# Fused attention and gated feed-forward on one core: places for split values, first queries in a rotary key's bank, a later copy of x, joined late transposes, last tokens tile by tile

## The chip, the cores and the metric

The kernel runs on 1 core of one Trainium2 chip. The metric is the device time of one execution in microseconds (us). The kernel before has a median of 2392.24 us over 3 runs (2391.26 to 2392.67).

## What is computed

One transformer layer on x with shape (2, 1024, 512). Attention has 32 query heads and 8 key and value heads of 128; keys are half rotary (from `Wkr`) and half made from a latent (`Wdk`, then `Wupk`), values come from the latent too (`Wupv`). The feed-forward part has 1376 hidden columns and weights packed in 4 bits.

```python
q = (x @ Wq.T).reshape(...)            # 32 heads, rotary
k_r = rotary(x @ Wkr.T)
c_kv = x @ Wdk.T
k_c, v = c_kv @ Wupk.T, c_kv @ Wupv.T  # 8 heads
attn = softmax(mask(q @ k.T / sqrt(128)))
x = layernorm(x + (attn @ v) @ Wo.T)
h = silu(x @ W1.T) * (x @ W3.T)
out = layernorm(x + h @ W2.T)
```

## The kernel before, in words

Every number is split into a high part (fp32r) and the low rest, and each product is three matmuls: high by high, high by low, low by high (`three_pass`, L262). Tokens come in four blocks of 512 (NBLK = 4, END = 3).

Phase A makes keys and values. For each block, TensorE makes four rotary key groups (RG + m), four latent key groups (NG + n) and eight value groups (VG + n) of 12 matmuls each, in a ring of eight PSUM banks (`a_bank`, L395). ScalarE takes the high part out of the bank (L991 for keys, L996 for values), VectorE the low part (L1246, L1251), and SyncE (SP) stores both (L617 `a_store_k`, L622 `a_store_v`). Rotary keys are turned by VectorE, and GpSimd (POOL) makes their low part (L892). Keys have four places in SBUF (`a_ks`), values two (`a_vs`); a place is used again when its store has landed (`a_k_out`, `a_v_out`). SP issues every transfer of the kernel, in one order written by hand: the parts of x of each block (L609), a copy of all of x to y in DRAM after block 0 (L820), keys and values of head group 0 in the third block (L667, L671), parts of x for the first queries (L674), sine and cosine (L830, L831), and so on.

Between A and B, for h in 0 to 3: late value group h (of the fourth block, h < V_LATE = 3), then queries h. The queries go into `banks[h % 2]`, which are the banks of latent keys 2 and 3. For each head ScalarE copies the two halves of the product swapped (L1032, L1033), POOL multiplies by sine (L897), VectorE by cosine (L1268), VectorE adds (L1275), ScalarE takes the high part (L1040) and VectorE, for these four, the low part (L1506).

Phase B has 16 turns (one for each batch and key head; turn 0 is "first", 1 to 14 a loop, 15 "last"), and a turn has 32 steps (CELLS), one for each query tile i = c // 4 and head h = c % 4. In step s TensorE computes the scores of cell s, transposes the normalised scores of cell s - 3 (LAG), and does a share of the "fill" (L77 to L95): queries for the next turn (q0, q1), products with the values (pv), with the output weights (wo) and, in turn 0, the late values 3 to 7 (va). `Plan` spreads the fill over the steps by the room of each (ROOM). Cells of query tiles 4 to 7 are transposed in two pieces, the first of four key tiles into one bank, the rest into the other (`pieces`, L55; `transposes`, L1610). A piece may be transposed when the scores are normalised (`norm_done`) and when VectorE has copied out the piece that was in this bank (`pt_lo`). In steps from 16 on the order on TensorE is scores, fill, piece 0, fill, piece 1, fill (PE_ORDER, L114), with the fill cut 1 : 1.25 : 1 (SHARES, L119; `turn_of`, L1790). ScalarE normalises (L1067), takes high parts (L1082) and exponentials (L1061) in the order of ACT_ORDER; VectorE adds the mask and finds the maximum (L1286) and takes low parts (L1304). The sum with x goes through y in DRAM (`load_y`, `store_y`, L676 to L682).

Phase C is the feed-forward part, four blocks. For each of the 11 hidden tiles f, TensorE does 24 up products (gate and up, L1638) and 12 down products (L1670), three for each of the four token tiles, which sum in four banks over all f. ScalarE takes silu (L1125) and the high part (L1128), VectorE the gate product (L1372) and the low part (L1378), into one of two places (`c_hs`). In the last block the down products of the last two tiles are ordered by token tile (`c_last_downs`, L1680); then VectorE adds the residual tile by tile (L1391) and takes statistics (L286), and one variance, one root (L305) and one chain of small steps (L312 to L320) serve the four tiles, before four scalings (L325) and three stores (L863).

```python
1826            for h in range(GQ):
1827                if h < V_LATE:
1828                    a_group(END, VG + h, a_values(END, h))
1829                if h < 2:
1830                    pe.wait_ge(a_bank_free, a_count(END, NG + 2 + h) + a_FREE0)
1831                else:
1832                    pe.wait_ge(q_cos, h - 1)
1833                queries(0, 0, h, h % 2, 0, products("q0", h))
```

Of the kernel before, what the change touches and what calls it, by code (L numbers as in the profile page):

```python
# [22 lines left out]
F32R = mybir.dt.float32r  # L23
# [95 lines left out]
SHARES = ((1,), (0, 1), (1, 1.25, 1))  # L119

# [151 lines left out]
class LayerNorm:  # L272
# [30 lines left out]
    def square_root(self, act, g):  # L303
        act.wait_ge(self.asked, g + 1)
        self.nc.scalar.activation(self.sd[:], self.var[:], ACT.Sqrt).then_inc(self.sqrt_done, 1)  # L305

    def reciprocal_root(self, dve, g):

        nc, var, sd, rs, tmp = self.nc, self.var[:], self.sd[:], self.rs[:], self.tmp[:]
# [23 lines left out]
def layer(nc, x, xT, wqT, wkrT, wdkT, wupkT, wupvT, woT, w13p, s13p, w2p, s2p, cosT, sinT, shifts,  # L333
# [5 lines left out]
    with ExitStack() as ctx:  # L339
# [22 lines left out]
        a_vs = at(164 * K, "a_vs", [P, 2, 4, 2, HD], F32R)  # L362
# [56 lines left out]
        a_v_out = [sem("a_v_out0"), sem("a_v_out1")]  # L419
# [167 lines left out]

        blocks_of_y = y_d.rearrange("b (h i) p d -> (b h) i p d", i=4)
# [4 lines left out]
        def _(sp):  # L593
# [26 lines left out]
            def a_store_v(t, n):  # L620
# [4 lines left out]
                    words(a_vs[:, n % 2]).rearrange("p g l d -> p g (l d)")).then_inc(a_v_out[n % 2], 16)  # L625

            def a_block_of(t):
# [150 lines left out]
            def turn_of(it, turn):  # L778
                for step in steps_of(turn):
# [40 lines left out]
            sp.dma_start(y_d.rearrange("b i p d -> (b i p) d"), x.rearrange("b s d -> (b s) d")).then_inc(a_y_out, 16)  # L820
# [11 lines left out]
            for n in range(8):  # L832
                a_store_k(END, n)
# [1082 lines left out]
```

## Time and profile before

| | |
|---|---|
| median of 3 runs | 2392.24 us |
| the profiled execution | 2391.44 us |
| its span, first to last instruction | 2389.7 us |
| mean granted TensorE clock | 0.997 |
| TensorE (PE) busy | 2366.3 us, 99% |
| weight loads (PEld) | 1988.7 us, 83% |
| ScalarE (ACT) | 1619.6 us, 68% |
| VectorE (DVE) | 1421.9 us, 60% |
| GpSimd (POOL) | 577.2 us, 24% |

Times in rows are counted from the start of the span. A matmul's duration in a row (0.39 us for 512 columns) is longer than the distance from one start to the next, because matmuls are pipelined; work is therefore counted from start to start. A row of the timeline merges neighbours of one kind: start, length, engine, line, operation, output and inputs, count, and in brackets the engine's idle time before it and what ended that. A few matmul records are missing from a trace, so a count can be one short.

### The profile page before, as it was taken

What the parts mean: (1) busy time and instruction counts of PE and PEld (TensorE: products, weight loads), DVE (VectorE), ACT (ScalarE), POOL (GpSimd) and SP (SyncE); (2) the same over time, 40 slices, a digit from 0 to 9 for tenths busy, and PEclk for the clock granted to TensorE, in tenths of its full rate; (3) what the DMA queues carried; (4) which work ended last, traced back from release to release, by engine and by line L of the source; (5) the groups of instructions that cost most, each with busy time, mean ns of one, the idle gap of its engine ahead of it and who ended that gap; (6) DMA issues with size and microseconds to landing.
All of it is one profiled execution on the core that took longest, in us unless ns stands there. A gap on an engine that the chain in (4) does not pass through costs nothing.

```text
span 2389.7 us, 40886 instructions
## 1 busy us (share of the span) xinstructions
PE 2366.3 (99%) x11999; PEld 1988.7 (83%) x11999; DVE 1421.9 (60%) x3781; ACT 1619.6 (68%) x3220; POOL 577.2 (24%) x451
## 2 busy tenths in 40 slices
PE   9998999999999999999999999999999999999998
PEld 8887888888888888888888888888888888888886
DVE  5334666676767676766667676766676665242332
ACT  4223878788888888887878888888888885122211
POOL 2101323233332323232323333232323220000000
PEclk9999999999999999999999999999999999999999
DMA  6787344444453544344444435354434445321110
GB/s 220 280 297 275 132 145 133 134 140 145 134 170 109 174 136 149 127 145 136 137 140 140 142 131 167 113 176 127 159 126 145 132 137 206 123 71 36 53 36 18
DMA packets 133256, 340.26 MB, mean 142 GB/s; under 512 B 13328, under 2 KB 30736, under 8 KB 122640
## 3 DMA queue, kind: packets, MB, share of 16 engines
q1 hardware_dynamic: 133200, 339.53, 42.5%
q8 instruction: 32, 0.52, 0.1%
q14 instruction: 24, 0.20, 0.0%
HBM read 232.00 MB, written 111.67 MB: 144 GB/s over the span
## 4 chain that ended last, share of the span: by engine, by line
PE 87%; DMA 1%; issue 1%; ACT 1%; DVE 1%; POOL 0%; SPq 0%; DVEq 0%; ACTq 0%; POOLq 0%
PE b_ps L267 43%; PE b_sps L267 28%; PE b_tps L1615 10%; PE b_ps L1674 3%; PE b_tps L1674 2%; DMA v_d<-a_vs 0%; DMA k_d<-a_ks 0%; ACT b_pt L1082 0%; DMA b_kt<-k_d 0%; PE b_sps L1624 0%; ACT b_sc L1067 0%; ACT b_sc L1061 0%; DMA y_d<-b_ys 0%; POOL b_sw L897 0%; DVE b_pt L1304 0%
## 5 line engine op out<-in xcount | busy, mean ns | idle before, releaser
L1304 DVE TENSOR_TENSOR b_pt<-b_tps,b_pt 128x512 fp32r<-128x512 f32 (+3 forms) x768 | 426.6, 556 | 302.2 <-ACT b_pt L1082 297.8
L267 PE MATMUL b_sps<-b_kt,b_qs 128*128 128x512 f32 (+4 forms) x2304 | 497.3, 343 | 1.3 <-DVE b_nmax L1286 1.0
L1067 ACT ACTIVATE b_sc<-b_sc,b_rinv 128x896 f32<-128x896 f32 (+7 forms) x512 | 396.1, 774 | 105.3 <-DVE b_rinv L1294 98.6
L267 PEld LDWEIGHTS b_sps<-b_kt,b_qs 128*128 128x128 f32 x2304 | 403.1, 188 | 57.8 <-issue 1.9
L267 PE MATMUL b_ps<-b_xs,b_wq 128*128 128x512 f32 x1536 | 443.1, 408 | 5.6 <-DVE a_ks L1246 5.6
L1082 ACT ACTIVATE b_pt<-b_tps 128x512 fp32r<-128x512 f32 (+3 forms) x768 | 367.5, 479 | 117.5 <-PE b_tps L1615 115.9
L267 PE MATMUL b_ps<-b_pt,b_vt 128*128 128x512 f32 x1584 | 436.2, 403 | 0.3 <-DVE b_ys L1315 0.3
L267 PE MATMUL b_ps<-b_wo,b_ot 128*128 128x512 f32 x1536 | 423.9, 405 | 0.1
L1061 ACT ACTIVATE b_sc<-b_sc,b_nmax 128x896 f32<-128x896 f32 (+7 forms) x512 | 395.4, 772 | 38.2 <-DVE b_nmax L1286 35.1
L1286 DVE CUSTOM_DVE_ANT_0 b_sc<-b_sps,b_mask 128x896 f32<-128x896 f32 (+7 forms) x512 | 386.4, 755 | 15.5 <-PE b_sps L267 15.4
L1615 PE MATMUL b_tps<-b_ident,b_sc 128*128 128x128 f32 x2304 | 374.5, 272 | 4.5 <-ACT b_sc L1067 2.9
L1615 PEld LDWEIGHTS b_tps<-b_ident,b_sc 128*128 128x128 f32 x2304 | 291.4, 140 | 80.2 <-issue 5.3
L267 PEld LDWEIGHTS b_ps<-b_pt,b_vt 128*128 128x128 f32 x1584 | 284.3, 188 | 49.0 <-DVE b_ys L1315 0.5
L267 PEld LDWEIGHTS b_ps<-b_xs,b_wq 128*128 128x128 f32 x1536 | 275.3, 190 | 51.6 <-DVE a_ks L1246 6.1
L267 PEld LDWEIGHTS b_ps<-b_wo,b_ot 128*128 128x128 f32 x1536 | 270.8, 189 | 43.5 <-DVE b_ys L1315 0.3
L897 POOL TENSOR_TENSOR b_sw<-b_sw,b_sin 128x512 f32<-128x512 f32 x128 | 165.7, 1295 | 374.9 <-ACT b_sw L1033 373.5
L901 POOL TENSOR_TENSOR b_qs<-b_qf,b_qs 128x512 fp32r<-128x512 f32 x124 | 160.3, 1293 | 395.0 <-ACT b_qs L1040 395.0
L267 PE MATMUL b_sps<-c_xs,c_up 128*128 128x512 f32 (+3 forms) x1056 | 247.5, 390 | 0.0
L267 PEld LDWEIGHTS b_sps<-c_xs,c_up 128*128 128x128 f32 (+1 forms) x1056 | 195.2, 185 | 43.7
L1372 DVE TENSOR_TENSOR c_hb<-b_sps,c_hb 128x512 f32<-128x512 f32 (+1 forms) x44 | 30.4, 691 | 193.4 <-PE b_sps L267 186.9
L1268 DVE TENSOR_TENSOR b_qf<-b_ps,b_cos 128x512 f32<-128x512 f32 x128 | 88.5, 691 | 90.8 <-ACT b_sw L1033 48.9
L910 POOL TENSOR_TENSOR b_wo<-b_wraw,b_wo 128x512 fp32r<-128x512 f32 x64 | 82.9, 1295 | 229.3 <-ACT b_wo L1055 229.3
(169 smaller groups left out, 2250.0 us busy)
## 6 DMA issues: line engine op xcount, KB each, us to landing
b_xs<-xs_d SPq DMA_DIRECT2D x32, 2048.0 KB, 9.3
b_ys<-y_d SPq DMA_DIRECT2D x128, 256.0 KB, 2.7
y_d<-b_ys SPq DMA_DIRECT2D x128, 256.0 KB, 3.0
b_wraw<-in_wqT SPq DMA_DIRECT2D x64, 256.0 KB, 2.8
k_d<-a_ks SPq DMA_DIRECT2D x32, 512.0 KB, 4.9
v_d<-a_vs SPq DMA_DIRECT2D x32, 512.0 KB, 3.2
b_kt<-k_d SPq DMA_DIRECT2D x64, 256.0 KB, 4.6
b_vt<-v_d SPq DMA_DIRECT2D x16, 1024.0 KB, 4.8
```

Of the source, the lines that this page charges most:

```text
L267: ins = nc.tensor.matmul(out, *every[n], start=(n == 0), stop=(n == len(every) - 1))
L897: nc.gpsimd.tensor_tensor(sw[:], sw[:], sinq[:, blk * TB:blk * TB + TB], ALU.mult).then_inc(sin_done, 1)
L901: nc.gpsimd.tensor_tensor(qs[:, blk, h, LO], qf[:], qs[:, blk, h, HI], ALU.subtract).then_inc(q_lo, 1)
L910: nc.gpsimd.tensor_tensor(wo[:, h, LO], wraw[:, h % 2], wo[:, h, HI], ALU.subtract).then_inc(w_lo, 1)
L1061: nc.scalar.activation(sc[:, slot, 0:w], sc[:, slot, 0:w], ACT.Exp, bias=nmax[:, slot:slot + 1], scale=-1.0, accum_out=rsum[:, slot:slot + ...
L1067: nc.scalar.activation(sc[:, slot, 0:w], sc[:, slot, 0:w], ACT.Copy, scale=rinv[:, slot:slot + 1])\
L1082: nc.scalar.activation(pt[:, u % PT_UNITS, HI, 0:nj, h * P:(h + 1) * P], tps[n % 2][:, 0:nj], ACT.Copy)\
L1268: nc.vector.tensor_tensor(qf[:], banks[bk], cosq[:, blk * TB:blk * TB + TB], ALU.mult)\
L1286: nc.vector.tensor_tensor_reduce(out=like_banks(sc[:, slot, 0:w], i), in0=both_banks(sps[c % 2], i), in1=like_banks(mask[:, S - w:S], i), ...
L1304: nc.vector.tensor_tensor(pt[:, u, LO, 0:nj, h * P:(h + 1) * P], tps[n % 2][:, 0:nj], pt[:, u, HI, 0:nj, h * P:(h + 1) * P], ALU.subtract) ...
L1615: last = nc.tensor.transpose(tps[n % 2][:, j], sc[:, c % S_RING, (j0 + j) * P:(j0 + j + 1) * P], ident[:])
L1674: last = nc.tensor.matmul(c_y[t], c_hs[0:w, f % 2, a, t * P:(t + 1) * P], c_w2[f][b][0:w], start=(f == 0 and k == 0), stop=(f == FT - 1 an ...
```

## The change

Values get four places, two of them where phase B has the values of a head group (8 and 12 KB); the first two query groups use the bank of rotary key 3 and come ahead of the late values; the copy of x to y is cut to the tiles that turn 0 does not read (nine of sixteen) and moves to step 13 of turn 0, which reads x itself; several transfers of SP move. From step 22 on the two pieces of a cell are transposed one right after the other. The last feed-forward block does all up products, then the down products token tile by token tile, with the hidden parts kept in the place of the up weights already used, and each token tile is normalised and stored by itself.

```diff
+JOINED = 22
+JOINED_ORDER, JOINED_SHARES = ("scores", "fill", 0, 1, "fill"), (1, 2.25)
...
+    def variance_of_tile(self, dve, g, t):
+        nc = self.nc
+        nc.vector.bn_stats(self.stats[:, t], self.tile(t)).then_inc(self.st, 1)
+        dve.wait_ge(self.st, 9 * g + 2 * t + 1)
+        nc.vector.bn_aggr(self.mv[:, t], self.stats[:, t]).then_inc(self.st, 1)
+        dve.wait_ge(self.st, 9 * g + 2 * t + 2)
+        nc.vector.tensor_scalar(self.var[:, t:t + 1], self.mv[:, t, 1:2], EPS, None, ALU.add).then_inc(self.asked, 1)
...
-    def square_root(self, act, g):
+    def square_root(self, act, g, t=0, width=4):
-    def reciprocal_root(self, dve, g):
+    def reciprocal_root(self, dve, g, t=0, width=4):
...
-        a_vs = at(164 * K, "a_vs", [P, 2, 4, 2, HD], F32R)
+        a_vs = [at(kb * K, f"a_vs{n}", [P, 4, 2, HD], F32R) for n, kb in enumerate((164, 168, 8, 12))]
...
+        def a_v_slot(t, n):
+            return n % 4 if t < END or n < 4 else n % 2
+        def a_v_uses(t, n):
+            return 2 * t + n // 4 if t < END or n < 4 else 2 * END + 1 + (n - 4) // 2
+        V_USES = [1 + max(a_v_uses(END, n) for n in range(8) if a_v_slot(END, n) == k) for k in range(4)]
+        Q_BANK = (3, 3, 0, 1)
...
+        y_rest, x_rest = (w[(QT - 1) * P:] for w in (y_d.rearrange("b i p d -> (b i p) d"),
+                                                     x.rearrange("b s d -> (b s) d")))
+        def c_h(n, f):
+            if type(n) is int and n == END:
+                return c_up[f][:].rearrange("q l m k c -> q (l m k c)")[:, 0:2 * TB].rearrange("q (l t) -> q l t", l=2)
+            return c_hs[:, f % 2]
...
             def a_block_of(t):
-                if t == END - 1:
-                    sp.wait_ge(a_fused, a_made(3, 3))
-                    for slot in range(4):
-                        sp.wait_ge(a_k_out[slot], 16 * 2 * 2)
-                    load_k(0)
                 for n in range(8):
-                    if t == END - 1 and n == 4:
-                        for p in range(2):
-                            sp.wait_ge(a_v_out[p], 16 * 4 * 2 + a_OUT0)
-                        load_v(0)
+                    if t == END - 1 and n == 7:
+                        sp.wait_ge(a_mm, a_count(END - 1, VG + 7) + a_MM0)
+                        sp.wait_ge(a_xs_out, 16 * END + a_OUT0)
+                        load_xs(0, 0)
                     a_store_v(t, n)
...
+                first = type(it) is int and it == 0
-                sp.dma_start(ys[:, i % 2], y_d[it // KV, i]).then_inc(y_in[i % 2], 16)
+                sp.dma_start(ys[:, i % 2], x_tiles[i] if first else y_d[it // KV, i]).then_inc(y_in[i % 2], 16)
...
+                    if step == 0 and turn == "loop":
+                        sp.wait_ge(a_y_out, 16)
+                    if turn == "first" and step == 5:
+                        for p in range(4):
+                            sp.wait_ge(a_v_out[p], 16 * (V_USES[p] if p >= 2 else 4) + a_OUT0)
+                        load_v(0)
+                    if turn == "first" and step == 6:
+                        a_store_x(END)
+                    if turn == "first" and step == 13:
+                        sp.dma_start(y_rest, x_rest).then_inc(a_y_out, 16)
...
             a_block_of(0)
-            sp.dma_start(y_d.rearrange("b i p d -> (b i p) d"), x.rearrange("b s d -> (b s) d")).then_inc(a_y_out, 16)
...
-            sp.wait_ge(a_mm, a_count(END - 1, VG + 7) + a_MM0)
-            sp.wait_ge(a_xs_out, 16 * END + a_OUT0)
-            load_xs(0, 0)
             sp.wait_ge(a_x_lo, END + a_XLO0)
-            sp.dma_start(sinq[:], sinT).then_inc(tab_in, 16)
-            sp.dma_start(cosq[:], cosT).then_inc(tab_in, 16)
             for n in range(8):
+                if n == 2:
+                    sp.dma_start(sinq[:], sinT).then_inc(tab_in, 16)
+                    sp.dma_start(cosq[:], cosT).then_inc(tab_in, 16)
+                if n == 4:
+                    load_k(0)
                 a_store_k(END, n)
             for n in range(V_LATE):
                 a_store_v(END, n)
             sp.wait_ge(q_mm, 4)
             load_xs(0, 1)
-            a_store_x(END)
...
-            for t, to in ((0, 2), (2, 3), (3, 4)):
+            for t in range(4):
+                sp.wait_ge(norm2.done, 4 * END + t + 1)
+                sp.dma_start(out[END, t], c_x1[:, t]).then_inc(c_o_out, 16)
...
             # ScalarE, between A and B (VectorE alike: queries, then the late value)
             for h in range(GQ):
+                swap_q(0, 0, h, Q_BANK[h])
+                hi_q(0, 0, h)
                 if h < V_LATE:
                     a_v_hi(END, h, a_bank[(VG + h) % a_RING])
-                swap_q(0, 0, h, h % 2)
-                hi_q(0, 0, h)
...
             def c_last_sum():
                 for t in range(4):
                     c_residual(END, (t,))
+                    dve.wait_ge(c_z_done, 4 * END + t + 1 + Z0)
+                    norm2.variance_of_tile(dve, END, t)
+                    norm2.reciprocal_root(dve, END, t, 1)
+                    norm2.scale_tiles((t,))
...
+            def c_last_block():
+                for index, (kind, what) in list(enumerate(ITEMS["last"]))[1:]:
+                    c_item(END, index, kind, what, "last")
+                pe.wait_ge(c_z_done, 4 * END + Z0)
+                for t in range(4):
+                    for f in range(FT):
+                        if t == 0:
+                            pe.wait_ge(c_h_lo, FT * END + f + 1 + HLO0)
+                        c_down_products(END, f, t)
...
-                    shares = cut(parts, SHARES[len(ts)])
-                    for job in (0, 1, "scores") if step == 0 else PE_ORDER[part_of(step)]:
+                    joined = step >= JOINED and len(ts) == 2
+                    shares = cut(parts, JOINED_SHARES if joined else SHARES[len(ts)])
+                    order = JOINED_ORDER if joined else PE_ORDER[part_of(step)]
+                    for job in (0, 1, "scores") if step == 0 else order:
...
             for h in range(GQ):
+                if h == 0:
+                    pe.wait_ge(a_bank_free, a_count(END, RG + 3) + a_FREE0)
+                elif h == 1:
+                    pe.wait_ge(q_cos, 1)
+                else:
+                    pe.wait_ge(a_bank_free, a_count(END, NG + h) + a_FREE0)
+                queries(0, 0, h, Q_BANK[h], 0, products("q0", h))
                 if h < V_LATE:
                     a_group(END, VG + h, a_values(END, h))
```

## Rows read from the trace of the kernel before

**Rows 1.** Windows of TensorE: us, busy us (matmuls), granted clock, DMA share, GB/s

```profile
194.00:222.00 28.00, 22.36 (x87) 0.88 0.62 226
222.00:245.00 23.00, 18.89 (x94) 1.00 0.82 290
245.00:2380.00 2135.00, 2132.59 (x10977) 1.00 0.39 128
```

**Rows 2.** List of waits: engine and line <- what it waited for: us, times, longest

```profile
ACT a_vs L996 <- DMA v_d<-a_vs: 39.2, 13, 11.0
...
PE b_tps L1615 <- ACT b_sc L1067: 2.9, 1, 2.9
```

**Rows 3.** Timeline of the opening, TensorE and VectorE

```profile
194.47 2.88 PE L267 MATMUL b_sps<-a_wupv,a_xe 128*128 128x512 f32 x12
...
202.99 5.49 PE L267 MATMUL b_ps<-b_xs,b_wq 128*128 128x512 f32 x12 [5.64 <-DVE a_ks L1246]
...
209.76 0.69 DVE L1268 TENSOR_TENSOR b_qf<-b_ps,b_cos 128x512 f32<-128x512 f32 x1 [4.93 <-ACT b_sw L1033]
...
222.07 0.39 PE L267 MATMUL b_ps<-a_wupv_hi,a_xe 128*128 128x512 f32 x1
```

**Rows 4.** Chain of waits in the opening: start, us, what

```profile
192.83 8.77 DMA k_d<-a_ks
...
223.55 0.60 ACT b_sw L1032
...
230.23 9.45 DMA v_d<-a_vs
```

**Rows 5.** DMA issues by kind: out<-in, count, KB each, median us to landing

```profile
b_xs<-xs_d SPq DMA_DIRECT2D x32, 2048.0 KB, 9.3
...
y_d<-in_x SPq DMA_DIRECT2D x1, 16.1
```

**Rows 6.** Timeline of TensorE, steps 3 and 4 of turn 0

```profile
234.06 1.32 PE L267 MATMUL b_ps<-b_xs,b_wq 128*128 128x512 f32 x5
```

**Rows 7.** Timeline of TensorE in the feed-forward blocks

```profile
2092.96 1.04 PE L1624 MATMUL b_sps<-b_ident,c_yb 128*128 128x128 f32 x8
...
2099.38 0.60 PE L1624 MATMUL b_sps<-b_ident,c_yb 128*128 128x128 f32 x4
...
2150.71 1.52 PE L1674 MATMUL b_ps<-c_w,c_hs 128*128 128x512 f32 x6
2152.07 1.03 PE L1624 MATMUL b_sps<-b_ident,c_yb 128*128 128x128 f32 x8
...
2158.43 1.52 PE L1674 MATMUL b_tps<-c_w,c_hs 128*128 128x512 f32 x6
```

**Rows 8.** Timeline of a turn, steps 24, 29 and 30: TensorE, and VectorE's copy

```profile
1184.04 1.39 PE L267 MATMUL b_sps<-b_kt,b_qs 128*128 128x448 f32 x6
...
1188.94 0.56 PE L267 MATMUL b_sps<-b_kt,b_qs 128*128 128x448 f32 x2
...
1207.48 1.53 PE L267 MATMUL b_sps<-b_kt,b_qs 128*128 128x512 f32 x6
...
1209.42 0.56 DVE L1304 TENSOR_TENSOR b_pt<-b_tps,b_pt 128x384 fp32r<-128x384 f32 x1 [1.08 <-ACT b_pt L1082]
...
1209.77 0.60 PE L1615 MATMUL b_tps<-b_ident,b_sc 128*128 128x128 f32 x4
...
1212.62 1.54 PE L267 MATMUL b_sps<-b_kt,b_qs 128*128 128x512 f32 x6
```

**Rows 9.** Timeline of the tail

```profile
2377.03 2.94 PE L1674 MATMUL b_ps<-c_w,c_hs 128*128 128x512 f32 x12
...
2380.01 0.69 DVE L1391 TENSOR_TENSOR c_x<-b_ps,c_x 128x512 f32<-128x512 f32 x1
...
2384.07 1.91 DVE L325 TENSOR_SCALAR c_x<-c_x,c_n_mv,c_n_rs 128x512 f32<-128x512 f32 x4
```

**Rows 10.** Stores of y, line 682: us from issue to landing, least, median, most

```profile
DMA to landing us min/median/max: 2.0/3.0/17.1
```

More of the change, by code:

```diff
@@ L418, in layer @@
         a_xs_out, a_y_out = sem("a_xs_out"), sem("a_y_out")
-        a_v_out = [sem("a_v_out0"), sem("a_v_out1")]
+        a_v_out = [sem(f"a_v_out{n}") for n in range(4)]
         tab_in, masked = sem("b_tab_in"), sem("b_masked")
@@ L824, in _ @@
                 a_block_of(t)
[L826 to L828 removed]
             sp.wait_ge(a_x_lo, END + a_XLO0)
[L830 to L831 removed]
+            sp.wait_ge(a_fused, a_made(3, 3))
+            for slot in range(4):
+                sp.wait_ge(a_k_out[slot], 16 * 2 * 2)
             for n in range(8):
+                if n == 2:
[3 more added lines that the diff above has]
+                    load_k(0)
                 a_store_k(END, n)
@@ L860, in _ @@
             c_block_io(END, True)
-            for t, to in ((0, 2), (2, 3), (3, 4)):
-                sp.wait_ge(norm2.done, 4 * END + to)
-                sp.dma_start(out[END, t:to].rearrange("i p d -> p i d"), c_x1[:, t:to]).then_inc(c_o_out, 16)
+            for t in range(4):
+                sp.wait_ge(norm2.done, 4 * END + t + 1)
+                sp.dma_start(out[END, t], c_x1[:, t]).then_inc(c_o_out, 16)
             sp.wait_ge(c_x1_out, 16 * NBLK)
-            sp.wait_ge(c_o_out, 16 * (NBLK + 2))
+            sp.wait_ge(c_o_out, 16 * (NBLK + 3))
         @block.gpsimd
@@ L949, in _ @@
             act.sem_inc(a_xs_out, a_OUT0)
-            act.sem_inc(a_v_out[0], a_OUT0)
-            act.sem_inc(a_v_out[1], a_OUT0)
+            for p in range(4):
+                act.sem_inc(a_v_out[p], a_OUT0)
             act.sem_inc(y_out[0], YO0)
@@ L1250, in a_v_lo @@
                 dve.wait_ge(a_part_hi, a_count(t, VG + n))
-                nc.vector.tensor_tensor(a_vs[:, n % 2, :, LO, :], ps.rearrange("p (g d) -> p g d", g=4),
-                                        a_vs[:, n % 2, :, HI, :], ALU.subtract).then_inc(a_bank_free, 1)
+                place = a_vs[a_v_slot(t, n)]
+                nc.vector.tensor_tensor(place[:, :, LO, :], ps.rearrange("p (g d) -> p g d", g=4),
+                                        place[:, :, HI, :], ALU.subtract).then_inc(a_bank_free, 1)
             def a_block_of(t):
@@ L1385, in c_residual @@
                         dve.wait_ge(c_x1_in, 16 * n + 16)
-                    if t < 3:
+                    if type(n) is int and n == END:
+                        dve.wait_ge(c_y_done, 3 * n + t + 1)
+                    elif t < 3:
                         dve.wait_ge(c_y_done, 3 * n + t + 1)
@@ L1701, in c_block_of @@
                         c_item(n, index, kind, what, place)
-                        if kind == "f" and (f < FT - 2 - (place == "last") or not todo):
+                        if kind == "f" and (f < FT - 2 or not todo):
                             break
@@ L1709, in c_block_of @@
                         pe.wait_ge(c_ab_free, PER)
-                    if f == FT - 1 and place != "last":
+                    if f == FT - 1:
                         c_item(n + 1, 0, "f", 0)
-                    if place == "last" and f == FT - 2:
-                        c_last_downs(n)
-                        break
                     if place != "first":
@@ L1826, in _ @@
             for h in range(GQ):
+                if h == 0:
[5 more added lines that the diff above has]
+                queries(0, 0, h, Q_BANK[h], 0, products("q0", h))
                 if h < V_LATE:
                     a_group(END, VG + h, a_values(END, h))
-                if h < 2:
-                    pe.wait_ge(a_bank_free, a_count(END, NG + 2 + h) + a_FREE0)
-                else:
-                    pe.wait_ge(q_cos, h - 1)
-                queries(0, 0, h, h % 2, 0, products("q0", h))
             turns(pe, turn_of)
@@ L1837, in _ @@
                 c_block_of(n, "next")
-            c_block_of(END, "last")
+            c_last_block()
 def kernel(L0_attn_hidden_states, L0_attn_Wq, L0_attn_Wkr, L0_attn_Wdk, L0_attn_Wupk, L0_attn_Wupv, L0_attn_Wo,
```

62 lines of the change are left out of this document (24 added, 38 removed).

## The prediction

> **What bounds the kernel now.** The windows of TensorE come first: from 245 to 2380 us it idles 2.4 of 2135 us. Between 194 and 245 us it idles 5.6 and 4.1 us [rows 1], and after 2380 us it has nothing left. So time can come from three places alone: this opening, the 9.7 us of the tail, and the spacing of TensorE's instructions in between. The list of waits names who was late: ScalarE waited 39.2 us for stores of values to land, and 2.9 us of TensorE stand against ScalarE's normalised scores [rows 2]. The timeline of the opening shows the first hole and its echo: a value group at 194.47 us, the first queries only at 202.99 us, behind VectorE's low parts of the keys, and these 12 products take 5.49 us where 12 take 2.7 elsewhere: after the idle stretch the granted clock had fallen to the lower of its two levels, 1.2 instead of 2.4 GHz. The late values of turn 0 begin at 222.07 us [rows 3]. The chain of waits says what was last: a key store that took 8.77 us to land, ScalarE's copy of queries 3 only at 223.55 us, a value store of 9.45 us [rows 4].
>
> All durations are of the profiled execution: span 2389.7 us, its own time 2391.44 us, 0.8 us under the median of 2392.24 us. I take the differences from the median.
>
> **Opening: 13.0 us before new costs.** Why does a store of 512 KB take 9 us, when one of 256 KB has a median of 3.0 [rows 10]? All transfers stand in SP's one list, and the large ones block it: the copy of x to y took 16.1 us, each 2 MB load of x parts 9.3 us [rows 5]. The change takes the 4 MB copy away from 87 us, moves the values of head group 0 (1 MB) from 172.8 us to step 5 and its keys (1 MB) behind the four rotary key stores, issues the 2 MB of x parts ahead of the third block's last value store and not at 184 us, and gives values four places for two. Up to 194 us TensorE has nothing to gain from that, since it is not in the list of waits there. But VectorE is no longer held by late values , so I expect rotary keys and their stores some 5 us sooner, and ScalarE through with the keys at about 195.5 us, just behind the last latent key group (194.47 us), instead of 203.5 us. Sine and cosine (1 MB, by the rate of rows 5 about 4.5 us) now stand ahead of the last two rotary stores; the 5 us cover them.
>
> The queries: the first product no longer needs a latent key's bank, only that of the fourth rotary key, which VectorE has left by then, so queries 0 go at 194.47 us. Queries 1 use the same bank and wait for the cosine of queries 0. Queries 0 now end about 208.5 and their cosine at 209.76 + 0.69 = 210.45 us [rows 3], 2.0 us later; the value group put between lasts 2.7 us, 0.7 us more. Seven groups of 12 at 2.72 us are 19.04 us; they took 222.07 - 194.47 = 27.60 us [rows 3]. Gain 8.6 us, the clock's 2.8 us among them.
>
> Next, ScalarE began on queries 3 at 223.55 us, 1.5 us after they were done, since it still had queries 2 in hand, and the mask and the third cell's scores followed late [rows 4]. With value group 2 between them this goes: 1.5 us. Late value 4 then waited for a store of 9.45 us that stood behind 2 MB of x in and 2 MB out [rows 4]; its new place was last used by value 0, and the store of x moves to step 6: the 2.9 us of TensorE go [rows 2]. Sum 8.6 + 1.5 + 2.9 = 13.0 us.
>
> **New queueing: costs 0.8 us (0 to 3).** The second load of x parts, issued right behind queries 3, takes 9.3 us [rows 5] and has a value store just ahead of it now; its first user comes about 10.5 us after queries 3 (234.06 - 222.07 is 12.0, less 1.5) [rows 6]: 0 to 0.5 us late. At step 5 SP waits until the places at 8 and 12 KB are stored, then loads the values over them; behind stand the store of x, value stores, and output weights wanted at step 11, some 12 us on. Value 7's place waits for the store of value 5 behind 3 MB: up to 1 us. The copy of the nine tiles left (2.4 MB) at step 13 takes 16.1 x 9/16 = 9 us and stands ahead of four loads of query weights and 2 MB of x parts; the third of these weights may come 2.5 us late for ScalarE. All exposed: 3 us. I take 0.8, near the lower end, as ScalarE has slack in these steps and TensorE follows it two steps behind. Net 12.2 us.
>
> **Transposes side by side: 6.0 us (0 to 10).** Six products of 512 columns last 1.36 us (2150.71 to 2152.07), 0.2267 us each [rows 7]; one transpose 0.1085 from start to start. Step 29 of a turn has 6 scores, 13 fills and 4 + 3 transposes: 19 x 0.2267 + 7 x 0.1085 = 5.07 us, and took 5.14 (1207.48 to 1212.62). Step 24 has 6 scores of 448 columns (in proportion 0.1984 each), 13 fills, 6 transposes: 4.79 us, and took 4.90 (1184.04 to 1188.94) [rows 8]. So two blocks of transposes cost 0.07 and 0.11 us beyond their parts, 0.09 in the mean. One block of eight, in the feed-forward part, with 24 products: 8 x 0.1085 + 24 x 0.2267 = 6.31 us, and took 6.36 (2152.07 to 2158.43) [rows 7]. A block costs 0.05 us, whatever its length. The change makes one block of two in ten steps (22 to 31) of 16 turns: 160 x 0.04 = 6.4 us, of which I take 6.0. Ends: another block of eight cost 0.11 us (2092.96 to 2099.38 is 6.42) [rows 7], no less than two blocks, so 0; and 0.11 - 0.05 = 0.06 us per step gives 10.
>
> Here a rule speaks against the change. The Trainium skill (TensorE: Matmul & The Clock Gate, section Back-to-back issue gap) gives a matmul's spacing as its columns over the clock plus 2.5 ns, with no price for a change of kind; by it the sum would be 6 us smaller. The trace does not agree: 227 ns for 512 columns against 216 ns by the rule, and 0.05 us per block.
>
> A joined second block also needs its bank copied out by VectorE since the step before: that ends at 1209.42 + 0.56 = 1209.98 us, and the block would start at 1209.77 + 4 x 0.1085 = 1210.20 us [rows 8]. The slack is 0.2 us in this step, the tightest that I found; cost 0.
>
> **Tail: 3.1 us (2.5 to 3.5).** The last block does its gate and up products in one run, then the down products tile by tile (33 each, 7.5 us): as many products as before. Sums, normalisation and stores of tiles 0 to 2 lie beside TensorE's work, 7.5 us for a chain of about 4. Now: products end at 2379.97 us, one sum at 2380.01, two statistics, one variance for four tiles, four scalings from 2384.07 to 2385.98, stores, end at 2389.70: 9.7 us [rows 9]. Then: sum 0.7, statistics 0.7, two small steps 0.4, root 0.3, five small steps 1.1 and one scaling 0.54 make 3.8 us; a 256 KB store lands in 2.0 us at best and 3.0 at the median [rows 10], here alone in the list, so 2.3; and 0.5 to the end: 6.6 us. Hidden parts live in the weights already used, so ScalarE waits for no down product; a gate of 0.7 us each 5.4 us leaves VectorE room for the block before.
>
> **Sum.** 12.2 + 6.0 + 3.1 = 21.3 us: 2392.24 - 21.3 = 2370.9, forecast 2371 us (span 2368.4).
>
> **Rivals.** (1) Grouping transposes gives nothing: for it the block at 2092.96 us, against it the one at 2152.07; the sum without its 6 us is 2377 us. Chance 0.17. (This is what the Trainium skill's rule above would do.) (2) In the opening one wait takes the other's place: rotary key stores still land 8.8 us late, ScalarE copies queries 0 at 203.5 us, and queries 1, bound to the same bank, start at 205.4 instead of 199.9 us; with the clock's fall 5.5 + 2.7 = 8.2 us are lost again: 2379 us. For it: sine, cosine and keys are still loaded in this stretch; against: the copy, the values and the 2 MB of x parts are out of the way by then. Chance 0.13. (3) Slower: joined second blocks wait for VectorE's copy. The slack is 0.2 us [rows 8]; beyond it 0.1 us in each of 160 steps costs 16 us, and from 0.1 us the 15 us of the rest are gone; at 0.25 us it is 40 - 15 = 25 us slower, 2417 us. For it: VectorE waits 1.08 us for ScalarE before that copy; against: ScalarE takes this piece behind its exponential in either order. Chance 0.03. (4) The early transfers are no cause of the holes and the regrouping does nothing: 2389 us by the tail alone, 0.04.
>
> **Numbers.** Forecast 0.63. Range 2366 (ten for the regrouping, no new cost) to 2379 us (rival 2 in full). A measurement tells about 0.2% (4.8 us) from no change: faster 0.94, same 0.03, slower 0.03.
>
> **What would show it.** Opening: no hole over 1 us from 190 to 245 us, granted clock 1.0 there, first late group near 213.5 us, ScalarE's wait for value stores under 15 us; wrong if TensorE waits for b_qf L1268. Turns 0.4 us shorter, step 29 at 5.11 us, no wait of transposes for b_pt L1304. Step 13: a wait for b_wraw under 3 us, ScalarE's alone. Tail: 6.6 us from last product to end. The forecast falls if the time between 245 and 2380 us keeps its length, or the half clock is seen again in the opening.

## The result, and the profile after

The changed kernel takes 2375.57 us (median of 4 runs, 2374.07 to 2376.76) beside 2391.75 us for the kernel of before (4 runs, 2390.52 to 2392.67): ratio 0.9932, 95% interval 0.9915 to 0.995. That is 16.2 us where 21.3 were forecast; the range of 2366 to 2379 us holds it. The profiled execution has a span of 2374.0 us (its own time 2375.78), 15.7 us less than before.

The windows of TensorE in the trace after (us, busy us and matmuls, granted clock, DMA share, GB/s):

```profile
194.00:222.00 28.00, 27.87 (x129) 1.00 0.71 243
222.00:245.00 23.00, 20.68 (x101) 0.93 0.75 260
245.00:280.00 35.00, 34.51 (x183) 1.00 0.68 228
280.00:1900.00 1620.00, 1618.89 (x8585) 1.00 0.42 141
1900.00:2020.00 120.00, 117.62 (x607) 1.00 0.47 171
```

The first line answers to the first of [rows 1]: the hole is gone and the clock stays up. The second idles 2.3 us where it idled 4.1, but the clock is below full there, and the two losses together are as large as before. The timeline of TensorE, and the chain of waits (start, us, what), tell both halves:

```profile
193.57 2.88 PE L269 MATMUL b_sps<-b_xs,b_wq 128*128 128x512 f32 x12
...
209.89 2.88 PE L269 MATMUL b_ps<-b_xs,b_wq 128*128 128x512 f32 x12
212.61 0.39 PE L269 MATMUL b_ps<-a_wupv_hi,a_xe 128*128 128x512 f32 x1
...
239.29 0.55 PE L1658 MATMUL b_tps<-b_ident,b_sc 128*128 128x128 f32 x3 [2.32 <-ACT b_sc L1108]
...
327.20 0.98 PE L269 MATMUL b_sps<-b_kt,b_qs 128*128 128x256 f32 x6
```

```profile
226.60 11.45 DMA v_d<-a_vs
...
238.13 0.60 ACT a_vs L1037
...
250.52 10.97 DMA b_wraw<-in_wqT
```

Seven groups take 212.61 - 193.57 = 19.04 us, and the first late group starts 9.5 us sooner than at 222.07 us [rows 3]. But the first scores of turn 1, at 336.60 us before and 327.20 us now, come only 9.4 us sooner: turn 0 gains nothing. The store of late value 5 lands 11.45 us after its issue, behind 1 MB of values in and 2 MB of x out. Late value 7 uses its place, ScalarE stands there, and normalised scores wait behind it: 2.32 us of TensorE. In the 4 us after that the granted clock is 0.57:

```profile
236.00:240.00 4.00, 1.68 (x10) 1.00 0.96 349
240.00:244.00 4.00, 4.00 (x13) 0.57 0.01 3
```

0.43 x 4 = 1.7 us more. The prediction had named both as signs against it: a hole over 1 us between 190 and 245 us, and the half clock seen again in the opening. In the list of waits (0 to 300 us) ScalarE's 39.2 us for value stores [rows 2] are down to 2.9 us, and there is a new wait for query weights, behind the copy that now stands at step 13:

```profile
ACT b_wq L1087 <- DMA b_wraw<-in_wqT: 3.2, 3, 2.3
ACT a_vs L1037 <- DMA v_d<-a_vs: 2.9, 1, 2.9
```

Steps 24 and 29 of a turn [rows 8] now take 4.86 us (1171.96 to 1176.82) and 5.13 us (1195.26 to 1200.39), where they took 4.90 and 5.14:

```profile
1171.96 1.38 PE L269 MATMUL b_sps<-b_kt,b_qs 128*128 128x448 f32 x6
...
1176.82 1.38 PE L269 MATMUL b_sps<-b_kt,b_qs 128*128 128x448 f32 x6
```

```profile
1195.26 1.52 PE L269 MATMUL b_sps<-b_kt,b_qs 128*128 128x512 f32 x6
...
1200.39 1.53 PE L269 MATMUL b_sps<-b_kt,b_qs 128*128 128x512 f32 x6
```

The tail [rows 9]: the last products end where the group of 17 does, 2363.77 + 4.03 = 2367.80 us, and the span at 2374.0, so 6.2 us for 9.7.

```profile
2363.77 4.03 PE L1717 MATMUL b_ps<-c_w,c_up 128*128 128x512 f32 x17
...
2367.84 0.69 DVE L1437 TENSOR_TENSOR c_x<-b_ps,c_x 128x512 f32<-128x512 f32 x1 [3.83 <-PE b_ps L1717]
...
2370.97 0.55 DVE L339 TENSOR_SCALAR c_x<-c_x,c_n_mv,c_n_rs 128x512 f32<-128x512 f32 x1
```

So the 15.7 us of the spans are 9.4 up to turn 1, 2.4 from there to the feed-forward part, and 3.9 in it and in the tail. Forecast were 12.2, 6.0 and 3.1.

### The profile page after: what moved, and what is told of

It is laid out like the page before. It is cut to its first block, busy times and chain, and to the rows that moved or that the text cites. A ratio compares the mean times of both kernels' runs of the same rounds, so it can differ in the third digit from the quotient of the medians.

```text
span 2374.0 us, 40892 instructions
## 1 busy us (share of the span) xinstructions
PE 2359.8 (99%) x11999; PEld 1994.7 (84%) x11999; DVE 1425.0 (60%) x3797; ACT 1619.1 (68%) x3223; POOL 577.5 (24%) x451
## 4 chain that ended last, share of the span: by engine, by line
PE 96%; DMA 2%; ACT 1%; DVE 1%; issue 0%; POOL 0%; SPq 0%; ACTq 0%; DVEq 0%; POOLq 0%
PE b_ps L269 45%; PE b_sps L269 32%; PE b_tps L1658 10%; PE b_tps L1717 3%; PE b_ps L1717 3%; PE b_tps L269 2%; DMA v_d<-a_vs 1%; DMA b_kt<-k_d 0%; DMA b_wraw<-in_wqT 0%; ACT b_sc L1102 0%; ACT b_sc L1108 0%; PE b_tps L1579 0%; PE b_sps L1667 0%; ACT b_pt L1123 0%; DVE b_sc L1330 0%
## 5 line engine op out<-in xcount | busy, mean ns | idle before, releaser
L1348 DVE TENSOR_TENSOR b_pt<-b_tps,b_pt 128x512 fp32r<-128x512 f32 (+3 forms) x768 | 426.4, 555 | 304.5 <-ACT b_pt L1123 300.3
L269 PE MATMUL b_ps<-b_pt,b_vt 128*128 128x512 f32 x1584 | 423.9, 399 | 0.3 <-DVE b_ys L1359 0.3
L269 PE MATMUL b_ps<-b_xs,b_wq 128*128 128x512 f32 x1512 | 418.7, 402 | 0.0
L269 PE MATMUL b_ps<-b_wo,b_ot 128*128 128x512 f32 x1536 | 415.6, 403 | 0.0
L1658 PE MATMUL b_tps<-b_ident,b_sc 128*128 128x128 f32 x2304 | 349.9, 273 | 4.5 <-ACT b_sc L1108 2.3
L1658 PEld LDWEIGHTS b_tps<-b_ident,b_sc 128*128 128x128 f32 x2304 | 282.8, 140 | 61.2 <-issue 5.3
```

Of the source, the lines that this page charges most:

```text
L269: ins = nc.tensor.matmul(out, *every[n], start=(n == 0), stop=(n == len(every) - 1))
L1348: nc.vector.tensor_tensor(pt[:, u, LO, 0:nj, h * P:(h + 1) * P], tps[n % 2][:, 0:nj], pt[:, u, HI, 0:nj, h * P:(h + 1) * P], ALU.subtract) ...
L1658: last = nc.tensor.transpose(tps[n % 2][:, j], sc[:, c % S_RING, (j0 + j) * P:(j0 + j + 1) * P], ident[:])
```

## The experiments

Each time stands beside the kernel of before on the same chip: 2391.58 us (21 runs) for e1 to e4, 2390.04 (9 runs) for e5 to e8, 2389.97 (15 runs) for e9 to e11, 2391.93 (7 runs) for e12. Single executions of one kernel spread over 0.4 to 5.4 us, and an interval of the ratio is 4 to 8 us wide in all, where most parts that are tried here are worth 1 to 4 us. So differences between medians decide little by themselves, and the profiles decide.

**e1: the old order of transposes.**

```diff
-JOINED = 22
+JOINED = 99
```

> The changed kernel with the transposes of steps 22 to 31 in the old order and the old shares. Theory A (read from the two traces: a turn became 0.25 to 0.3 us shorter, of which the last four steps save 0.04 us each and the steps before them less, and the last turn gained about 1 us of small holes): slower than the changed kernel by 3 to 4 us, 2379.1 us, with turns back at 111.15 us. Theory B (the forecast, 0.04 us in each of 160 steps): slower by 6.0 us, 2381.6 us. Theory C (regrouping gives nothing, the turns became shorter for another reason): 2375.6 us and turns still at 110.9 us.

2377.59 us, ratio 0.9945 (0.9932 to 0.9959): 2.0 us slower than the changed kernel, 2.2 if each is taken from its own kernel of before. That is below A's 3 to 4 and B's 6, though these medians alone don't exclude either.

**e3: the new order alone, in the kernel of before** (the same lines of the diff, without the rest).

> The kernel of before with the regrouped transposes alone (steps 22 to 31 of every turn). Theory A: 4 us faster than before, 2387.8 us, turns 0.25 to 0.3 us shorter, small holes of about 1 us in the last turn. Theory B (the forecast): 6.0 us faster, 2385.8 us. Theory C: no gain, 2391.8 us.

2389.67 us (11 runs), ratio 0.9992 (0.9983 to 1.0001): 1.9 us faster, not clear of no change by the times. I then split each turn in the four traces at its first scores and its last. In the 13 turns after turn 1 the part between them takes 103.12 to 103.21 us before and 102.93 to 102.98 us after; with order back it is 103.10 to 103.21, with order alone 102.93 to 102.99. So regrouping is worth 0.20 us a turn, and that is sharp. What is left of a turn, from its last scores to the next turn's first, scatters from 7.8 to 8.7 us in all four kernels, and was once 9.6. And in the last turn regrouping costs 0.7 us of idle time, as the windows from 1900 us show, of before, of order alone, and of order back:

```profile
1900.00:2020.00 120.00, 118.28 (x619) 1.00 0.41 142
```

```profile
1900.00:2020.00 120.00, 117.56 (x612) 1.00 0.42 150
```

```profile
1900.00:2020.00 120.00, 118.21 (x609) 1.00 0.47 175
```

There transposes wait for VectorE's copy, 1.9 us in 5 waits (L1348) for 1.3 us in 4 before: the mechanism of rival 3, in one turn with short steps. From its first scores to its last this turn takes 93.42 us in the changed kernel and 92.51 before. 15 x 0.20 - 0.9 = 2.1 us, beside 1.9 and 2.0 measured.

**e6: regrouped in steps 28 to 31 only, and not in the last turn.**

```diff
-JOINED = 22
+JOINED = 28
...
-                    joined = step >= JOINED and len(ts) == 2
+                    joined = step >= JOINED and len(ts) == 2 and turn != "last"
```

> The changed kernel with the regrouped transposes in steps 28 to 31 only and not in the last turn. Theory A (only the last four steps save anything, 0.04 us each and the turn's start 0.03; in the last turn joined second blocks wait for VectorE, 0.7 us in all): from first to last scores a turn takes 102.95 to 103.00 us as in the changed kernel, the last turn's TensorE idle time between 1900 and 2020 us falls from 2.4 to 1.7 us, 0.3 to 0.7 us faster than the changed kernel, 2375 us. Theory B (all ten steps save alike, 0.02 us each): a turn takes 103.07 us, 1 us slower in all, 2376.6 us.

2376.82 us, ratio 0.9942 (0.9928 to 0.9956): 1.2 us slower than the changed kernel, 3.0 if each is taken from its own kernel of before, so the times can't choose between the theories. Between its first and last scores a turn now takes 103.05 to 103.11 us in 11 of 13 turns (two were longer): B. Four steps save some 0.07 us of 0.20, as they would if all ten save 0.02 alike. The last turn's idle time did fall to 1.75 us.

**e4: the new last block alone**, in the kernel of before.

> The kernel of before with the new last block alone (gate and up products in one run, down products tile by tile, each tile normalised and stored by itself). Theory A (the tail alone changes): from the last product to the end 6.2 to 6.6 us in place of 9.7, 3.1 to 3.5 us faster, 2388.5 us. Theory B (the order of the last block also costs or gives TensorE time): the sum of the block's products differs from before by over 0.5 us and the total gain lies outside 2.5 to 4 us.

2387.51 us (11 runs), ratio 0.9984 (0.9975 to 0.9993): 4.1 us faster, a little over A's 3.5 and over B's bound of 4, but the interval reaches from 1.7 to 6.0 us. In the trace it is A: its last product ends at 2380.45 us of a span of 2386.6, 6.15 us. From the last wait of the last turn to the last product it is 376.54 us, 376.94 before and 376.56 in the changed kernel: 3.5 us of tail and 0.4 us ahead of it.

**e2: the store of x parts behind value 5's.**

```diff
-                    if turn == "first" and step == 6:
-                        a_store_x(END)
...
                             a_store_v(END, a)
+                            if a == 5:
+                                a_store_x(END)
```

> The changed kernel with the 2 MB store of x parts behind the store of late value 5 and no longer ahead of it. Theory A (late value 7 waited for the store of value 5, which stood behind values in and x out, and TensorE lost 2.3 us there and about 1.6 us of half clock after it): the store of value 5 lands near 232.5 us in place of 237.8, the hole at 236.7 us is gone, the granted clock stays 1.0 from 194 to 262 us, and the time is 3.9 us shorter, 2371.7 us. Theory B (the hole only moves: the output weights and the store of value 6 stand behind the 2 MB instead, and ScalarE waits for them before it copies output weights): no gain within 1 us, 2375.6 us, with a hole of about 2 us between 238 and 250 us.

2374.88 us, ratio 0.993 (0.9917 to 0.9944): 0.7 us faster than the changed kernel (0.5 beside before), not 3.9. The hole and the half clock are gone, and so far A is right, though value 5's store landed at 234.88 us and not near 232.5; but 1.3 us more is lost in the next window:

```profile
222.00:245.00 23.00, 22.94 (x120) 1.00 0.75 274
245.00:280.00 35.00, 33.22 (x175) 1.00 0.67 222
```

```profile
ACT b_wq L1087 <- DMA b_wraw<-in_wqT: 2.7, 2, 1.5
```

TensorE arrives sooner at the query weights, which stand behind the copy of nine tiles. That is B in kind, in another place than it said. And at turn 1 TensorE waits 1.7 us for the keys, of which more below.

Theory A's 3.9 us was also taken from one execution. e1, e5 and e6 issue the same transfers in the same order up to there, and their profiles show the hole at 1.49 to 1.57 us with no half clock, but more idle time in the next window. These are e5's:

```profile
222.00:245.00 23.00, 21.51 (x113) 1.00 0.75 274
245.00:280.00 35.00, 33.22 (x177) 1.00 0.67 223
```

In all, e1, e5 and e6 idle 3.0 to 3.3 us between 222 and 280 us, e2 1.8 us.

**e7: the copy back at 87 us, on top of e2.**

```diff
-                    if turn == "first" and step == 13:
-                        sp.dma_start(y_rest, x_rest).then_inc(a_y_out, 16)
...
             a_block_of(0)
+            sp.dma_start(y_rest, x_rest).then_inc(a_y_out, 16)
             load_wq(0, 2)
```

> The kernel with the store of x parts later, and with the copy of nine tiles of x to y back behind the first block's stores (87 us) in place of step 13. Theory A (the copy at step 13 makes query weights late: TensorE idle 1.8 us between 245 and 280 us): these holes go, the opening to 194 us is no longer, 1 to 1.8 us faster than that kernel, 2373.5 us. Theory B (the early copy was what made the rotary key stores late at 190 us): a hole of some us comes back at 194 to 205 us and the time is 3 to 8 us longer, 2378 us or more. Theory C (the holes come from the 2 MB of x parts and not from the copy): no change within 0.5 us.

2370.72 us (2369.89 to 2371.0), ratio 0.9918 (0.9904 to 0.9931): 19.3 us faster than before, where e2 had 16.7 (the intervals of the two overlap). In the trace, A:

```profile
222.00:245.00 23.00, 23.00 (x120) 1.00 0.77 280
245.00:280.00 35.00, 35.00 (x191) 1.00 0.49 162
```

The 1.8 us of e2's idle time are gone, and up to 280 us no wait over 0.2 us is left. The move to step 13 cost time and brought none; nine tiles at 87 us don't disturb the opening.

**e8: banks and order of the first queries as before.**

```diff
-        Q_BANK = (3, 3, 0, 1)
+        Q_BANK = (0, 1, 0, 1)
```

and each late value group ahead of its queries again, on the three engines.

> The changed kernel with the first queries back in the banks of before, (0, 1, 0, 1), and each of the three late value groups again ahead of its queries; the four places for values and the moved transfers stay. Theory A (the transfers alone held the keys up; the latent keys now leave their banks at 193.6 and 195.6 us): no hole at 194 to 205 us, first late group of turn 0 still near 213 us, at most 1.5 us slower by the third cell, 2375.6 to 2377 us. Theory B (the bank and the order are what removes the hole): a hole of 3 to 6 us comes back at 197 us with half the clock behind it, 2380 to 2384 us.

2376.81 us (4 runs), ratio 0.9942 (0.9927 to 0.9957). A: no hole at 197 us. The one place up to 222 us where it waits is the third cell's scores, 0.95 us (as in the trace of before) against my 1.5:

```profile
220.20 0.59 PE L269 MATMUL b_sps<-b_kt,b_qs 128*128 128x256 f32 x3 [0.95 <-DVE b_nmax L1330]
```

By the medians e8 is 1.2 us slower than the changed kernel, and 3.0 if each is taken from its own kernel of before, against A's 1.5 at most. The profiled execution was the slowest of its four (2380.9 us); it has the hole behind value 5's store too (2.47 us up to 241.78, half the clock after it) and one of 1.56 us at 272 us. How much of that belongs to the banks isn't shown.

**e10: two places for values**, on top of e7.

```diff
-            return n % 4 if t < END or n < 4 else n % 2
+            return n % 2
...
-            return 2 * t + n // 4 if t < END or n < 4 else 2 * END + 1 + (n - 4) // 2
+            return 4 * t + n // 2
```

> The kernel with store of x parts later and the copy early, but two places for values in place of four; all transfers stay where the change put them. Theory A (the order of the transfers alone makes the stores short: with nothing of 1 to 4 MB ahead of them they land in about 3 us, and two places are enough): ScalarE's waits for value stores under 3 us between 100 and 200 us, no hole over 1 us at 194 to 210 us, within 1 us of the kernel with four places, 2370.7 us. Theory B (the places are what frees ScalarE and VectorE for the rotary keys): waits for value stores of 10 us and more, the hole comes back at about 196 us and half a clock behind it, 5 to 9 us slower, 2376 to 2380 us.

2371.36 us (4 runs), ratio 0.9921 (0.9905 to 0.9936): 18.6 us faster than before. A in the time, half A in the waits: ScalarE waits four times what A allowed, and TensorE does not wait for it.

```profile
ACT a_vs L1036 <- DMA v_d<-a_vs: 12.3, 6, 5.0
```

**e12: keys and values of group 0 back in the third block**, on top of e10: the two loads and their waits at the places that the change took them from.

> The kernel with two places for values, the copy early and the store of x parts later, but with the keys (1 MB) and the values (1 MB) of head group 0 again loaded in the third block's stores, as before the change; the 2 MB of x parts stay ahead of that block's last value store. Theory A (these two loads, ahead of value stores that ScalarE waits for, are what made the whole list late up to 200 us): ScalarE waits for value stores 25 us and more between 100 and 222 us, the x parts are issued near 182 us in place of 172.3, and TensorE idles 4 to 6 us near 197 us with half a clock behind it, 6 to 8 us slower than with two places alone, 2377.5 to 2379.5 us. Theory B (the x parts' place and the order of the rotary stores carry it): no hole over 1 us at 194 to 210 us, within 1 us of 2371.4 us.

2370.78 us (4 runs, 2369.59 to 2374.73; the slowest is the profiled one), ratio 0.9909 (0.9892 to 0.9925): 21.2 us faster than before. My theory A falls: ScalarE waits 26.8 us for value stores, as it said, and TensorE has no hole up to 280 us.

```profile
ACT a_vs L1036 <- DMA v_d<-a_vs: 26.8, 12, 5.2
...
ACT a_xs L1011 <- DMA a_xraw<-in_xT: 2.7, 1, 2.7
```

The same two lines of the kernel of before, in the same window of 100 to 222 us:

```profile
ACT a_vs L996 <- DMA v_d<-a_vs: 34.2, 12, 11.0
...
ACT a_xs L971 <- DMA a_xraw<-in_xT: 8.4, 1, 8.4
```

The last line points at what is left: ScalarE got the next block's x at 108.5 us before, 8.4 us late, and gets it at 103.1 us here, 2.7 us late. The copy at 87 us was 4 MB and took 16.1 us [rows 5]; here it is 2304 KB and takes some 11 us, and seven tiles of x go to their users straight from the input:

```profile
y_d<-in_x SPq DMA_DIRECT2D x1, 2304.0 KB, 11.6
```

(This row is e7's, with the copy in the same place.) The last value store of the second block was issued at 139.1 us before, at 131.9 us in e12; the 2 MB of x parts at 184.1 and 175.4 us. So the list ran 5 to 9 us late from the copy on, and the x parts ahead of a value store keep it short at the end.

The wait that made the first hole was one for stores of keys, though, not of values. A latent key's high part needs the place of a rotary key, and the stores of the four rotary keys stood behind the 2 MB of x parts and behind sine and cosine. ScalarE's first latent key of this block, before and in e12:

```profile
199.06 0.60 ACT L991 ACTIVATE a_ks<-b_tps 128x512 fp32r<-128x512 f32 x1 [7.02 <-DMA k_d<-a_ks]
```

```profile
188.65 0.60 ACT L1031 ACTIVATE a_ks<-b_tps 128x512 fp32r<-128x512 f32 x1 [1.24 <-DMA k_d<-a_ks]
```

The first rotary store was issued at 188.93 us before and took 10.1 us; in e12 it goes at 182.81 us and takes 5.8. Three parts of the change are in every kernel without the hole, then: the smaller copy, the x parts ahead of a value store, and sine and cosine behind the first two rotary stores. Which of the three does most wasn't tried, and stays open.

**e5: three products more between the last scores of a turn and the next keys.**

```diff
-        11, 7]
+        8, 7]
```

(the room of step 30; step 31 takes what is over)

> The changed kernel with three products moved from step 30 to step 31 of a turn, so that 0.68 us more of TensorE's work lies between the last scores of a turn and the first of the next. Theory A (each turn start waits for the four loads of keys: in the changed kernel the stretch from the last scores to the first of the next turn took 7.81 to 8.67 us, mean 8.02, while without a wait it would take 7.81): the stretch becomes 8.49 us in all turns but the worst, the rest of the turn 102.27 us, and 15 turns gain 0.2 us each, some 2 to 3 us: 2373 us, with less spread from run to run. Theory B (TensorE is not held by the keys, the spread of the stretch is noise of its own): the stretch keeps a spread of 0.9 us above 8.49, no gain, 2375.6 us; it may lose where the softmax of step 30 has less cover.

2373.43 us (2372.29 to 2375.31), ratio 0.9932 (0.9918 to 0.9945). In the trace A is right to the digit. Six last scores of a turn and the first of the next, of the changed kernel in a usual turn and in its worst, and of e5 in two turns:

```profile
428.97 1.53 PE L269 MATMUL b_sps<-b_kt,b_qs 128*128 128x512 f32 x6
...
437.98 0.73 PE L269 MATMUL b_sps<-b_kt,b_qs 128*128 128x256 f32 x4
...
1205.05 1.53 PE L269 MATMUL b_sps<-b_kt,b_qs 128*128 128x512 f32 x6
...
1214.87 0.38 PE L269 MATMUL b_sps<-b_kt,b_qs 128*128 128x256 f32 x1 [0.62 <-DMA b_kt<-k_d]
```

```profile
427.76 1.54 PE L269 MATMUL b_sps<-b_kt,b_qs 128*128 128x512 f32 x6
...
437.40 0.96 PE L269 MATMUL b_sps<-b_kt,b_qs 128*128 128x256 f32 x6
...
1203.06 1.54 PE L269 MATMUL b_sps<-b_kt,b_qs 128*128 128x512 f32 x6
...
1212.70 0.96 PE L269 MATMUL b_sps<-b_kt,b_qs 128*128 128x256 f32 x6
```

9.01 and 9.82 us in the one, 9.64 and 9.64 us in the other (counted from the last of the six, 1.14 us less: 7.87 and 8.68, then 8.49). All 15 stretches of e5 are 8.49 us; those of the changed kernel are 7.81 to 8.67, mean 8.01. In 14 of its 15 turns the first scores start 0.22 to 0.27 us after the fourth load of keys has landed, however long that took: they wait for it. In e5 it landed 0.7 to 1.3 us ahead of them. The profile's list of waits gives TensorE 1.1 us in two waits for this, between 280 and 1900 us; my split of the turns gives 15 x (8.01 - 7.81) = 3.0 us. The gain in time is less sharp than in the trace, 16.6 us to before where the changed kernel had 16.2, and its runs spread no less (3.0 us for 2.7): this opening, held by the same two transfers, had 1.5 us of hole at 237 us and 1.4 at 260 us.

**e11: the same in the kernel of before.**

> The kernel of before with nothing but three products moved from step 30 to step 31. Theory A (its turn starts too were held by the key loads: 8.00 us in the mean, 7.84 at least): all starts at 8.52 us, 15 x 0.16 = 2.4 us faster than before, and its own runs closer together. Theory B (only the changed kernel is on that edge): no gain, 2391 us.

2388.55 us (11 runs), ratio 0.9993 (0.9984 to 1.0002): 1.4 us, not clear of no change by the times. All its stretches are 8.54 us, so before was on that edge too. Its runs still spread over 2.9 us, so there is another source of spread; the holes of the opening, which differ from profile to profile, are a likely one.

**e9: together.** e7, with e5's room and with the old order in the last turn.

> The store of x parts later, the copy of x to y early, three products moved from step 30 to 31, and the transposes regrouped in all turns but the last. Theory A (the parts add up: the kernel with the early copy had turn starts of 7.90 us in the mean where 7.81 would do, so 15 x 0.09 = 1.4 us, and 0.7 us of waits in the last turn go): 2.1 us faster than that kernel, 2368.6 us beside a kernel of before at 2390.0 us, all turn starts at 8.49 us. Theory B (one of the new places is used up: with the turns ahead of their keys, the softmax of step 30 or the loads of query weights become late): no faster than 2370.7 us, with TensorE idle over 1 us between 280 and 1900 us.

2369.15 us (2368.96 to 2369.36, 4 runs), ratio 0.9911 (0.9896 to 0.9926): 20.8 us faster than before, 4.6 more than the change (the intervals still overlap). All turn starts are 8.49 us, the last turn idles 1.75 us instead of 2.4, and four executions lie within 0.4 us. What is late next, between 280 and 1900 us:

```profile
PE b_ps L269 <- DMA b_xs<-xs_d: 1.1, 1, 1.1
PE b_tps L1657 <- DVE b_pt L1347: 0.6, 1, 0.6
```

B happened once: at 327 us queries wait for x parts, for 1.1 us, and turn 1 takes 104.79 us from first to last scores where the others take 102.26. The gain over e7 is 1.5 us (20.8 for 19.3) and not 2.1, a difference that the times can't settle.

## Why the prediction was right, and where it was off

The side and the range held, and the opening was the largest term; the sum was 5 us too large. The tail, forecast at half of the regrouping, brought more than it. And one of the signs by which the forecast was to fall did come: the half clock was seen again in the opening.

**First hole and its clock, 8.6 us: right.** Seven groups in 19.04 us, no half clock up to 222 us, ScalarE's wait for value stores under 15 us, and ScalarE through with the keys at 194.9 us (forecast 195.5). The first group also starts 0.9 us sooner, at 193.57 us; that is luck, since it starts anywhere from 193.6 to 194.7 us in the fourteen traces, in kernels of both kinds. **Its cause was told too widely.** The prediction gave the rotary keys' lateness to all large transfers and to late values on VectorE, and the queries' own start to the new bank. e8, e10 and e12 take the bank, the four places and the later loads of group 0 away in turn, and no hole comes back. No run takes all three away together. What was left in all of them is the smaller copy, the x parts ahead of a store, and sine and cosine behind two rotary stores.

**Third cell, 1.5 us:** 0.95 of it is idle time, before and in e8. **Value 4's store, 2.9 us:** gone, but a like wait stands in its place.

**New queueing, 0.8 us (0 to 3): this step failed.** "Value 7's place waits for the store of value 5 behind 3 MB: up to 1 us" was 2.3 us, and I priced the wait alone, without the clock that falls behind it (1.7 us), although [rows 3] show just that pair. With 0.4 us for query weights it is 4.4 us, beyond my upper end, and it eats the 1.5 + 2.9 us of the step before. The clock's part is not there in every execution: e1, e5 and e6, with the same list, keep the full clock and idle 3.0 to 3.3 us, at my upper end or just above it. A bound by rows was at hand: 2 MB take 9.3 us, so 3 MB some 14 us by the rate of [rows 5], and the place was wanted 8.6 us after its store's issue (ScalarE stood from 235.2 us); e2 takes the wait away, e7 the one behind the copy.

**Transposes side by side, 6.0 us (0 to 10): the right kind, and nearly three times too large.** I took 0.05 us for a block "whatever its length" from blocks in the feed-forward part. In the turns one block less saves 0.02 us in each step, all ten alike (e6), not 0.04: 3.0 us. The last turn gives 0.7 to 0.9 back, against the sign "no wait of transposes for b_pt"; step 29 took 5.13 us and not 5.11. The rule of the Trainium skill (TensorE: Matmul & The Clock Gate, section Back-to-back issue gap), which has no price for a change of kind, is off by these 0.20 us a turn; the trace lies between it and my forecast. That section of the Trainium skill calls the spacing an isolated one and gives 131 ns for 512 columns in a sustained stream; here it is 227 ns, so neither figure fits. Rival 1, no gain at all, is out by the split of the turns, not by the times alone.

**Tail, 3.1 us (2.5 to 3.5): 3.9.** 6.2 us for the forecast 6.6 (I gave the last store 2.3 us), and 0.4 us that I had not seen ahead of it, as the down products of a tile stand together.

**What I missed in the profile of before:** "from 245 to 2380 us it idles 2.4 us" is true of the rows and still hid 2.2 us (15 x (7.99 - 7.84)) in which TensorE waited for keys. It changed no term, since both kernels have it, but any gain ahead of a turn's last scores counts, and none in the stretch after them.

Rivals 2 and 4 did not come: no wait for the cosine, and the first hole did close.

## What to carry over

A transfer that is moved out of a hole takes a new place in the list: ask what is issued right behind it, and when that is wanted, and price the clock's fall with a wait where the rows show one. Look for waits that show no idle time, by comparing when a transfer lands with when its user starts in every turn: the same distance each time, while the landing itself scatters, is a wait. Try each part of a change by itself even when the whole is a gain: here the copy's move cost 1.8 us of idle time (2.6 us by the medians), the regrouping 0.7 us in one turn of 16, and taking back the four places, the new bank or the two moved loads did not open the hole again.

## What was not expected of the hardware

A short wait leaves no idle time in the records. A matmul of 128 columns has 0.27 us in its row and the next can start 0.03 us after it started; so when the scores came 0.17 us late (7.98 us for 7.81), the profile shows TensorE busy throughout. The four key loads of one turn, all the same size, took 6.7 to 7.6 us from the first issue to the last landing in the changed kernel, and 8.1 to 8.6 us at the first turn start in e2, e3, e6 and e12. In the profiled executions turns 2 to 14 last 110.74 to 111.64 us in the changed kernel, and 110.72 to 110.77 us in e5, where TensorE does not wait for these loads. Next, whether the granted clock fell after a hole of this size did not go by its length. It fell to half after 2.32 us (236.97 to 239.29 us) in the changed kernel, after 2.47 us in e8 and after 2.52 us in e11. It did not after 2.91 us in the trace of before [rows 2], 3.27 us in e4 or 2.52 us in e3. These are the 4 us behind the hole in e11 and before:

```profile
239.00:243.00 4.00, 4.00 (x14) 0.57 0.83 262
```

```profile
241.00:245.00 4.00, 3.89 (x20) 1.00 0.74 223
```

After the holes of 1.5 us in e1, e5 and e6 it stayed at full. Why it fell after some and not after others stays open; e11's part of the list is that of before, so it is not the kernel alone that decides. Last, a store issued behind 3 MB landed 11.45 us later, though it is 512 KB itself. The Trainium skill (DMA: Bandwidth & Descriptors, section Queues, rings and completion order) says that each DMA engine takes descriptors in the order of the ring; the trace agrees: the values landed at 231.76 us, the x parts at 236.69, the store at 238.05, in the order of their issue. In e2, with only the 1 MB ahead of it, the same store took 8.63 us.
